# Attention with three banks for scores and two for shifted products, issued half a step apart

## The reference, cut to what matters

```
x = x + tanh(g_xattn) * cross_attention(layernorm(x), ctx)      # 32 heads of 8, axial rotary positions
    logits = q k^T / sqrt(8);  w = softmax(logits);  attn = w v;  attn @ Wout + bout
x = x + tanh(g_ffn) * moe(layernorm(x))
    2 shared experts / 2  +  6 of 32 routed experts (softmax gates), each relu(x w1 + b1) w2 + b2, hidden 176
```

## Time and profile before

| | |
|---|---|
| median of three runs | 456.51 us |
| the profiled execution | 453.48 us, of which 451.5 us is the span that the trace shows |
| granted TensorE clock, mean | 0.97 |
| TensorE busy (matmul) | 426.4 us, 94% |
| VectorE busy | 279.4 us, 62% |
| ScalarE busy | 192.3 us, 43% |
| GpSimd busy | 141.9 us, 31% |
| share of the chain that ended last | TensorE 83%, VectorE 10% |
| row maxima L766 on VectorE | 128 of 686 ns |
| exponentials L509 on ScalarE | 128 of 605 ns |

### The profile page before, as it was taken

How to read it: one execution, slowest core, us unless ns; L and a number is a source line. 1 busy time by engine, 2 the same in 40 slices (tenths; PEclk the granted TensorE clock), 3 DMA queues, 4 the chain that set the end, 5 groups by cost and what they waited for, 6 DMA issues and landing times.

```text
span 451.5 us, 8155 instructions
## 1 busy us (share of the span) xinstructions
PE 426.4 (94%) x2617; PEld 322.5 (71%) x2617; DVE 279.4 (62%) x589; ACT 192.3 (43%) x371; POOL 141.9 (31%) x231
## 2 busy tenths in 40 slices
PE   7778999999999987999999999999999999999996
PEld 5556665665656556776888888888888888888884
DVE  7988788679789734635455555555555444455454
ACT  4784788668777742622222222222222222222221
POOL 8369100000000010532444444333333344444430
PEclk9995899699999998999999999999999999999999
DMA  7200000000000007939995323333333343333102
GB/s 217 79 1 1 1 1 2 1 0 4 0 2 1 1 1 196 316 86 272 338 250 139 93 93 93 93 94 93 95 98 102 102 107 93 99 93 93 46 0 93
DMA packets 27960, 39.41 MB, mean 87 GB/s; under 512 B 3634, under 2 KB 22114, under 8 KB 27938
## 3 DMA queue, kind: packets, MB, share of 16 engines
q1 hardware_dynamic: 26897, 39.11, 30.8%
q10 hardware_dynamic: 1040, 0.01, 0.1%
HBM read 37.93 MB, written 1.18 MB: 87 GB/s over the span
## 4 chain that ended last, share of the span: by engine, by line
PE 83%; DVE 10%; issue 2%; ACT 2%; DMA 1%; SPq 0%; DVEq 0%
PE psum L1195 28%; PE psum L1212 28%; PE psum L1015 7%; PE psum L1064 7%; DVE nmax L766 5%; PE psum L1115 2%; PE psum L1049 2%; PE psum L996 2%; PE psum L1077 1%; PE psum L921 1%; DMA x_sb<-in_x_dram 1%; DVE attn L781 1%; PE psum L961 1%; PE psum L1250 1%; PE psum L1029 1%
## 5 line engine op out<-in xcount | busy, mean ns | idle before, releaser
L612 ACT ACTIVATE hh<-hu 128x512 fp32r<-128x512 f32 x88 | 55.6, 633 | 186.6 <-DVE hu L890 186.6
L890 DVE SCALAR_TENSOR_TENSOR hu<-psum,b1cols,G 128x512 f32<-128x512 f32 x88 | 65.8, 750 | 109.6 <-PE psum L1195 99.2
L766 DVE TENSOR_REDUCE nmax<-psum 128x2 f32<-128x512 f32 x128 | 82.3, 686 | 12.1 <-PE psum L1015 10.6
L509 ACT ACTIVATE probs<-psum 128x512 f32<-128x512 f32 x128 | 70.3, 605 | 26.7 <-PE psum L1029 26.3
L1212 PE MATMUL psum<-hh,w2h 128*128 128x512 f32 (+1 forms) x188 | 73.3, 390 | 0.0
L1212 PE MATMUL psum<-hh,w2l 128*128 128x512 f32 (+1 forms) x188 | 73.2, 389 | 0.0
L1212 PE MATMUL psum<-hl,w2h 128*128 128x512 f32 (+1 forms) x188 | 73.1, 389 | 0.0
L896 DVE SCALAR_TENSOR_TENSOR hl<-hu,hh 128x512 fp32r<-128x512 f32 x88 | 61.1, 697 | 9.1 <-ACT hh L612 9.1
L428 POOL CAST w2h<-w 128x256 fp32r x44 | 18.4, 419 | 129.9 <-PE psum L1212 129.9
L1195 PE MATMUL psum<-xTh,w1h 128*128 128x512 f32 (+1 forms) x188 | 58.2, 391 | 0.0
L1195 PE MATMUL psum<-xTl,w1h 128*128 128x512 f32 (+1 forms) x188 | 58.0, 389 | 0.0
(11 more groups left out here) (146 smaller groups left out, 519.7 us busy)
## 6 DMA issues: line engine op xcount, KB each, us to landing
G<-gates_by_expert SPq DMA_DIRECT2D x40, 256.0 KB, 3.9
w<-in_L_ffn_rw_dram SPq DMA_DIRECT2D x4, 1408.0 KB, 11.4
w<-in_L_ffn_rw_dram SPq DMA_DIRECT2D x2, 2816.0 KB, 18.2
G<-gates_by_expert SPq DMA_DIRECT2D x8, 448.0 KB, 3.6
G<-gates_by_expert SPq DMA_DIRECT2D x8, 384.0 KB, 3.5
G<-gates_by_expert SPq DMA_DIRECT2D x8, 320.0 KB, 3.5
G<-gates_by_expert SPq DMA_DIRECT2D x8, 192.0 KB, 3.7
x_sb<-in_x_dram SPq DMA_DIRECT2D x4, 256.0 KB, 4.5
```

The lines of the kernel that those rows point to most:

```text
L509: act.activation(probs[g % 2][:, :, n, :], ST_BANK[(4 * g + n) % 3][:, :].rearrange("p (t q) -> p t q", t=TB), ACT.Exp, scale=SCALE).then_ ...
L612: act.activation(hh[(SHT + j) % 2][:, cols], hu[2 * j + half][:, :], ACT.Relu).then_inc(rhh_ok, 1)
L766: dve.tensor_reduce(nmax[i % 2][:, :, SCORE_HEADS[n]], S_BANK[n % 2][:, :].rearrange("p (t k) -> p t k", t=TB), AX.X, ALU.max, negate=True ...
L890: dve.scalar_tensor_tensor(out=hu[2 * (j % 2) + half][:, :], in0=H_BANK[2 * (j % 2) + half], scalar=b1cols[:, bass.ds(it * len(G) + j, 1)] ...
```

## The change

- Three banks for scores (`SB`), taken in turn over all heads; two for shifted products (`STB`). The heads of a group are now scored in the order 0, 1, 2, 3 (before 2, 3, 0, 1), and `QK` has five buffers instead of four.
- Order of a step on TensorE: scores 0, 1, 2 of group i with shifted products 2 and 3 of group i-3; L1049; L996; score 3 with shifted products 0 and 1 of group i-2; values of group i-3. The exponentials on ScalarE move along.
- The extra steps' transposes and projections go to `T_BANK`. The next `transposes` waits for them to be read; ScalarE copies its `QK` earlier in those steps, and `attnT` at the start of the next step.
- Fillers: 8 instead of 2 ahead of the first scores, 6 at the end of each of steps 0, 1 and 2; none any more in steps 33 and 34; 2 instead of 4 ahead of the last projection.
- VectorE: the variances of the second layer norm are taken a step earlier, and the last `normalise` comes before the reciprocal roots and the six normalised rows, not behind them.

```diff
-WARM_UP, WARM_START = 7, 2
+WARM_UP, WARM_START, WARM_FILL = 7, 8, 6
...
-    RING, AHEAD = 4, 2
+    RING, AHEAD = 5, 2
...
-        S_BANK, ST_BANK, O_BANK, T_BANK, T2_BANK = banks[0:2], banks[2:5], banks[5], banks[6], banks[7]
-        C_AT, C_PJ = T2_BANK, [[T2_BANK, T2_BANK] for b in range(B - 1)] + [[T2_BANK, T_BANK]]
+        S_BANK, ST_BANK, O_BANK, T_BANK, T2_BANK = banks[0:3], banks[3:5], banks[5], banks[6], banks[7]
+        C_AT = [T_BANK] * (B - 1) + [T2_BANK]
+        C_PJ = [[T_BANK, T_BANK] for b in range(B - 1)] + [[T2_BANK, T_BANK]]
...
             def step(i):
-                g = i - 2
-                if 0 <= g < GROUPS:
-                    for n in range(3):
-                        exponentials(g, n)
+                g, late = i - 2, i - 3
+                busy = i in ATTN_STEPS or i in PROJ_STEPS
+                if i - 1 in ATTN_STEPS:
+                    transposed_attention(ATTN_STEPS.index(i - 1))
+                if 0 <= late < GROUPS:
+                    exponentials(late, 2)
+                    exponentials(late, 3)
                 if 0 <= i - 1 < GROUPS:
                     queries_with_max(i - 1)
+                if busy and i + AHEAD < GROUPS:
+                    evacuate_t(i + AHEAD)
                 if 0 <= g < GROUPS:
-                    exponentials(g, 3)
-                if i + AHEAD < GROUPS:
+                    exponentials(g, 0)
+                    exponentials(g, 1)
+                if not busy and i + AHEAD < GROUPS:
                     evacuate_t(i + AHEAD)
...
-                if i == GROUPS + 2:
+                if i == GROUPS + 1:
                     variances(0, NT - TB)
-                    inverse_deviations(0, NT - TB)
-
-
+
+
+            normalise(PAIRS - 1)
+            inverse_deviations(0, NT - TB)
             for b in range(B - 1):
                 normalise_rows(b, xn2[:, b], xn2_ok)
-            normalise(PAIRS - 1)
...
-                    if qt == 0 and 4 * i + n >= 2:
-                        pe.wait_ge(s_max, 4 * i + n - 1)
+                    if qt == 0 and 4 * i + n >= SB:
+                        pe.wait_ge(s_max, 4 * i + n - SB + 1)
...
-                    if kt == 0 and 4 * i + n >= 3:
-                        pe.wait_ge(exp_ok, 4 * i + n - 2)
+                    if kt == 0 and 4 * i + n >= STB:
+                        pe.wait_ge(exp_ok, 4 * i + n - STB + 1)
...
-                if new and shifted:
-                    pairs(score(i, 0), shifted_score(i - 2, 0))
-                    pairs(score(i, 1), shifted_score(i - 2, 1), shifted_score(i - 2, 2))
+                if new and weighted:
+                    pairs(score(i, 0), shifted_score(i - 3, 2))
+                    pairs(score(i, 1), shifted_score(i - 3, 3))
+                    pairs(score(i, 2))
...
                 if new and shifted:
-                    pairs(score(i, 2), shifted_score(i - 2, 3))
-                    pairs(score(i, 3))
+                    pairs(score(i, 3), shifted_score(i - 2, 0))
+                    pairs(shifted_score(i - 2, 1))
...
                 if weighted:
                     values(i - 3)
+                else:
+                    keep_warm(WARM_FILL, O_BANK)
...
-                if i > GROUPS:
-                    keep_warm(3, S_BANK[0])
...
-            keep_warm(4, S_BANK[0])
+            keep_warm(2, S_BANK[0])
```

More of the change, by code:

```diff
@@ L230, in gated_cross_attention_moe @@
         PROJ_STEPS = {NG * (b + 1) + 6 + 2 * t: (b, t) for b in range(B - 1) for t in range(TB)}
-        SCORE_HEADS = [(n + GH // 2) % GH for n in range(GH)]
+        SB, STB = len(S_BANK), len(ST_BANK)
         xf = x.rearrange("b (t p) d -> p (b t) d", p=P)
@@ L538, in transposed_attention @@
                     act.wait_ge(pj_mm, TB * (b - 1))
-                act.activation(attnT[b % 2], C_AT.rearrange("p (t k q) -> p t k q", t=TB, k=KD), ACT.Copy).then_inc(aT_ok, 1)
+                act.activation(attnT[b % 2], C_AT[b].rearrange("p (t k q) -> p t k q", t=TB, k=KD), ACT.Copy).then_inc(aT_ok, 1)
             for i in range(GROUPS + 3):
@@ L1041, in transposed_with_max @@
                     pe.wait_ge(norm_ok, (i - 3) // 2)
-                for b_done, step in enumerate(ATTN_STEPS):
-                    if i == step:
-                        pe.wait_ge(aT_ok, b_done + 1)
-                if i in PROJ_STEPS:
-                    b_done, t = PROJ_STEPS[i]
-                    pe.wait_ge(pj_ok, TB * b_done + t + 1)
                 for t in range(TB):
@@ L1104, in attention_transposed @@
                         n = (t * KD + k) * P
-                        ins = pe.transpose(C_AT[:, n:n + P], attn[:, TB * b + t, k * P:(k + 1) * P], ident[:, :])
+                        ins = pe.transpose(C_AT[b][:, n:n + P], attn[:, TB * b + t, k * P:(k + 1) * P], ident[:, :])
                 ins.then_inc(aT_mm, 1)
@@ L1120, in _ @@
                 new, shifted, weighted = i < GROUPS, 0 <= i - 2 < GROUPS, 0 <= i - 3 < GROUPS
-                if new and shifted:
-                    pairs(score(i, 0), shifted_score(i - 2, 0))
-                    pairs(score(i, 1), shifted_score(i - 2, 1), shifted_score(i - 2, 2))
+                if new and weighted:
+                    pairs(score(i, 0), shifted_score(i - 3, 2))
+                    pairs(score(i, 1), shifted_score(i - 3, 3))
+                    pairs(score(i, 2))
                 elif new:
-                    pairs(score(i, 0), score(i, 1))
-                elif shifted:
-                    pairs(shifted_score(i - 2, 0), shifted_score(i - 2, 1))
-                    pairs(shifted_score(i - 2, 2))
+                    pairs(score(i, 0), score(i, 1), score(i, 2))
+                elif weighted:
+                    pairs(shifted_score(i - 3, 2), shifted_score(i - 3, 3))
                 if 0 <= i - 1 < GROUPS:
@@ L1133, in _ @@
                 if new and shifted:
-                    pairs(score(i, 2), shifted_score(i - 2, 3))
-                    pairs(score(i, 3))
+                    pairs(score(i, 3), shifted_score(i - 2, 0))
+                    pairs(shifted_score(i - 2, 1))
                 elif new:
-                    pairs(score(i, 2))
                     pairs(score(i, 3))
                 elif shifted:
-                    pairs(shifted_score(i - 2, 3))
+                    pairs(shifted_score(i - 2, 0))
+                    pairs(shifted_score(i - 2, 1))
                 if weighted:
                     values(i - 3)
+                else:
+                    keep_warm(WARM_FILL, O_BANK)
                 if i >= 5 and i % 2:
```

27 lines of the change are left out of this document (15 added, 12 removed).

## The result

The changed kernel took a median of **440.2 us** (four runs, 439.32 to 446.33); the kernel before, on the same chip, 455.8 (four runs, 454.83 to 468.48). The forecast was 441.5. The profiled executions compare as 453.48 with 440.06: 13.4 us, where 14.9 were forecast.

A forecast was written before the change was run, and what follows sets the result against it. TensorE's program order, with a wait for VectorE in its middle, was taken to pace the attention pair. Gains 8.9 + 2.9 + 3.1 = 14.9 took the profiled 453.5 to 438.6, median 441.5 us; range 433 to 452.

The forecast's parts named there:

- The middle: 27 attention steps, maxima of step 5 to end of last maxima: 107.1 us to 98.2, with pairs of 6.65; gain 8.9.
- ScalarE starts 0.57 behind the first half: Steady attention step: exponentials start 0.57 us behind the first half, so the second ends 1.65 behind the step's head.
- The extra steps: Attention steps with added projections or transposes: 1.4 us for each of five projections, 0.6 for each of three transposes.
- Exponentials take the place of the maxima's wait: Steady step on TensorE: the 0.30 us wait for a row maximum goes; shifted product 1 waits up to 0.3 for an exponential.
- Rival 3: Freed banks do nothing in the attention: pairs stay at 7.25, 7.8 us of gain lost, 449 us; chance 0.13.
- rival 4: Attention slower: values wait for both late exponentials, 0.97 us a step, deciding from about 0.6; 466 us; chance 0.07.
- Filling: Attention steps 0 to 4: 19.9 us become 17.0 at full clock held by fillers; gain 2.9.
- Drain: Last maxima to last residual: last `normalise` 11.3 us behind the maxima instead of 13.2, gain 1.9, then 1.2 more; gain 3.1.
- without the gap of 2.52 the clock should not fall: Drain, last `normalise` to last residual: no clock fall, and two fillers fewer; gain 1.2 us, between 0.5 and 1.8.
- Rival 1: Clock falls all the same, at the filling or later: +2 to +8 us, likeliest +4.5, 446 us; chance 0.2.
- The offset of 3.0: Whole kernel: the profiled execution is 3.0 us under the median (453.5 against 456.5), assumed to stay the same.
- The floor of 6.39: Attention: VectorE needs at least 2 x 2.91 + 0.57 = 6.39 us for a pair of steps.

The follow-up runs named there:

- half exponentials: Changed kernel with each exponential over 256 of its 512 columns, part of the softmax left out: 435.4 us (one run).
- the weights later: Changed kernel with the three loads of the second half of the routed experts' weights on SyncE behind gate rows 8, 11 and 14: 439.7 us, ratio 0.964.
- both moves: Changed kernel with L1006 ahead of L1053 on TensorE, and `oT` copied on ScalarE in the odd step behind the late exponentials: 441.1 us, ratio 0.967.
- without fillers: Changed kernel with 2 fillers ahead of the first scores and none in steps 0, 1 and 2: 444.1 us, ratio 0.968.
- the fillers alone: Kernel before plus 8 fillers ahead of the first scores and 6 in steps 0, 1 and 2, its banks, order and drain kept: 455.35 us, ratio 0.986.

## Why the prediction was right, step by step

- **The middle, 8.9 forecast, 9.0 measured**, but as the sum of two misses. The steady pair is 6.8, not 6.65. The step that was off: "ScalarE starts 0.57 behind the first half". In the new order ScalarE is not free at the head of an odd step, and it is still at its `QK` and `oT` copies: the first late exponential starts 0.85 behind the head (97.92 to 98.77) and the second ends 0.3 later than forecast. Moving `oT` alone gave 0.58, and pairs of 6.65 and 6.71. That is 13 x 0.15 = 2.0 too little. The extra steps were cheaper by as much: a projection step's residual and its wait (0.55 to 0.78 in the changed kernel) lie in part in the time in which the pair waits for exponentials anyway, so the two were not to be added. The pair from step 16 to step 18, with two extra steps, takes 7.78 in the changed kernel and 7.79 with half exponentials, where the steady pairs differ by 0.5. With half exponentials, where the pair has no such wait, the 27 steps take 93.75: less 13 x 6.27 and 2.9 that leaves 9.3 for the extra steps, near the 8.8 of the forecast; in the changed kernel it leaves 98.1 - 88.4 - 2.9 = 6.8.
- **Exponentials take the place of the maxima's wait:** right, and shown from both sides, by halving exponentials (6.27) and maxima (6.8). Rival 3, pairs of 7.25, is out. So is rival 4: values are held up in odd steps only, by 1.10 - 0.44 = 0.66, which is 0.33 a step, under its point of 0.6.
- **Filling, 2.9 forecast, 3.4 measured:** at full clock its steps are 3.4, 3.4, 3.5, 3.2 and 3.1 (between the maxima at 31.87, 35.24, 38.68, 42.14, 45.30 and 48.41); the 0.5 added for the small writes was not needed.
- **Drain, 3.1 forecast, 1.7 measured.** The step that failed: "without the gap of 2.52 the clock should not fall". It fell, at 158 us:

```profile
158.00:160.00 2.00, 1.94 (x10) 1.65 (x9) 1.83 (x10) 0.00 (x0) 0.12 (x1) 0.50 0.12 12
```

  and the same two microseconds with the weights later, where TensorE's program up to there is the same:

```profile
158.00:160.00 2.00, 1.43 (x11) 1.15 (x10) 1.86 (x10) 0.60 (x1) 0.11 (x1) 1.00 0.26 38
```

  There the drain took 15.6 us, a gain of 2.7. So 1.1 of the missing 1.4 is the clock. The other term that was off is the last `normalise`: it ended 12.1 us behind the last maxima in both, where 11.3 was forecast, so this part gained 1.1 and not 1.9; from there to the last residual 1.6 was gained where the clock held, more than the 1.2 forecast. What was not seen: the gap of 2.52 was gone, but waits of 0.78, 1.17 and 0.51 for ScalarE had come in front of shifted products, values and L1079 (151.94, 155.81, 157.38).
- **Experts' stretch, forecast unchanged, 1.0 longer:** the fifth gate row came 6.5 us late for VectorE. A wait of 5.9 was there before and cost nothing; 0.6 more reached TensorE. That the shorter attention is the cause is not shown. SyncE issued this row 10.2 us behind the first product with b2, against 9.9 before (200.51 and 214.43), and in kernels with the same order of issue on SyncE the wait lay between 2.6 (both moves) and 9.1 us (without fillers). It was 8.5 with the fillers alone, whose attention is no shorter. A part of this 1.0 may be chance.
- **The clock.** Rival 1 (it falls all the same) is half true: not in 47 to 145 us, where it was 1.00, but in the drain here, and in the filling in the profiled runs of two kernels with the same fillers. The rule that was weighed, of the Trainium skill's TensorE: Matmul & The Clock Gate (section "A second HAM failure mode: psum-queue depth-cycling"), was borne out by the kernel with two banks for scores, whose clock lay at 0.57; for the changed kernel's own waits, 0.2 to 0.6 us long from 47 to 145 us, it did not come true.
- The offset of 3.0 between median and profiled execution did not carry over: 440.2 against 440.06. The gain was put 1.5 us too high and the offset 2.9, with opposite effect on the sum, which leaves the forecast of the median 1.3 too high: that it lies so near is in part luck.
- Two slips in the working, neither of weight: 438.6 and 3.0 make 441.6, not 441.5; and the trace of the kernel before shows the half level not twice but a third time, at the end of the gap of 2.52 (granted clock 0.52 from 172.0 to 175.5 us).

## What to carry to other kernels

When a bank is moved from one use to another, find the engine that frees the other use and read what stands ahead of that work in its program: here one small copy decided the last 0.13 us of a pair. An order of issue and the number of banks that it needs are to be tried together; the new order without the bank was some 60 to 70 us slower. And a few microseconds won ahead of a stretch that TensorE fills can be hidden by its scatter, here 246.9 to 251.7 us over the traces, from a late transfer and from the clock.

## What the runs showed of the hardware

- The clock fell at or right behind the products with b2 in seven of thirteen traces (that of the kernel with two banks for scores is not counted), with TensorE busy in every microsecond from 182 to 200. What ran there were eight products on 34 rows of the array. It fell so in all six traces in which the clock had stayed at 1.00 from 47 us up to these products, and in one of the seven others. The cause is open; no experiment was made on it.
- The fillers did not keep the clock in every run: 0.55 and 0.76 from 33 to 47 us in two profiled executions, 1.00 in the nine others with the same fillers (again without the two-bank kernel).
- Four row maxima in a row took 2.48 us instead of 2.57 to 2.67, each still 684 ns long. This is a wait and not a pace of VectorE. Before, the third started 0.67 to 0.78 behind the second, and 0.60 in the changed kernel; the other two intervals are 0.60 to 0.61 in both. With two banks the third score cannot be written before the first maximum is taken (in the earlier trace rows it starts at 108.83, the first maximum ends at 108.77), so it comes a little late for VectorE, by less than the shortest wait that the profile prints. The floor of 6.39 in the prediction has these waits in it; without them it is 2.89 + 3.40 = 6.29, as with half exponentials.
